# The second norm and the first group's queries of a one-core decoder kernel, in another order

## The chip, the cores and the metric

One Trainium2 chip, one of its cores. The metric is the device time of one execution in microseconds; the kernel before has a median of 811.94 us over 3 runs (811.52 to 813.64). A core has these engines, each with an instruction queue of its own: TensorE (PE, matrix products), VectorE (DVE), ScalarE (ACT), GpSimd (POOL) and SyncE (SP, which here only issues DMAs). They wait for one another on semaphores.

## The reference

One decoder layer on x of shape 16 x 64 x 512 (16 sequences of 64 tokens, 1024 tokens in all), with three parts:

```
x = x + attn(layernorm(x))        # here attn(h) = h + a softmax mix over the 16 sequences, per channel
x = x + xattn(layernorm(x), ctx)  # 32 query heads, 8 key/value heads of 128, RMS norm on queries and keys
x = x + moe(layernorm(x))         # 16 experts, 4 per token, and a shared one

q = rmsnorm(h @ Wq.T); k = rmsnorm(ctx @ Wk.T); v = ctx @ Wv.T
out = softmax(q k^T / sqrt(128) + mask) v @ Wo.T
```

The change lies at the seam of the first and second parts: the second layernorm, the transposes of its rows, and the projection of the first of eight groups of heads.

## The kernel before, in words

Products of 32-bit values are made of three products of 16-bit halves (hi x hi, hi x lo, lo x hi). So nearly every operand is split: ACT writes a high part (a 16-bit copy), then DVE or POOL subtracts it and writes the low part. Both must be there before PE can run the three products. A projection of 128 rows of weights against 512 tokens has 4 chunks, so it is 12 matmuls (`product`, L1740).

**First part, until about 56 us.** x lies as `xh`: 128 partitions (2 channel halves x 64 positions) by 16 sequences by 256 channels. DVE adds the messages of the first attention (L1236), and from the fourth of eight on `x1_done` allows more; statistics of the rows follow (L1242, L1246, L1155). PE swaps the halves' statistics by a small matmul (L2073); meanwhile it projects keys (`project_k`) and the first half of the values (`project_v(0, 0, 6, ...)`, L2070 and L2075) of group 0.

**Second norm.** ACT computes the scales (L736, L738). Then ACT normalises the rows of sequences 1, 3, ..., 11 (`ACT_ROWS`, L749) and DVE the ten others (`DVE_ROWS`, L1191) into `h2`. PE transposes them, two sequences to a tile of 128 tokens, 8 tiles (`transpose_rows`, L1817 to L1827): tile t waits for rows 2t and 2t + 1, and from t = 4 on for the low part of tile t - 4, because four PSUM banks are used in turn. ACT writes the high part (`transposed_hi`), DVE the low part (`transposed_lo`, L1252).

**First group.** `iteration(-1, False, True)` on PE (L1976 on) has 8 units u of queries: head u // 2 and half u % 2 of the tokens, in bank 4 + u % 2. Unit u >= 2 waits until the low part of unit u - 2 has been made from the same bank (`q_split`, L1865). Before unit 0 it waits for 4 low parts of tiles, before unit 1 for 8. After the units PE projects the second half of the values (L2023), then sums squares. The sums of the key squares, which give the keys' scale, come before unit 0 (L2079, half 0) and behind it (L2009, half 1), both in bank 7.

On ACT a unit is `q_parts` (L826): the query's high part (L830), its square (L834), the square's high part (L836). Beside the units each step k of the first group holds one piece of an expert weight that is split and written to `w_split` in DRAM (`first_hi(4 + k)`, L922), and the rest of the key path is laid into steps by hand:

```
L950  if k == 1: k_scale(p, 1, 7)            # ACT
L952  if k in (3, 4): k_hi_part(p, k - 3)
L954  if k == 7: v_hi_part(p, 1, 7)
L1407 if k in (1, 2): key_norm(p, k - 1)     # DVE, each behind q_lo_part and pre_lo(4 + k)
L1409 if k in (4, 5): key_lo(p, k - 4)
L1411 if k == 7: v_lo_part(p, 1, 7)
```

`k_scale` (two ACT operations) of half 0 stands before the units (L1042). DVE's step is `q_lo_part` (L1277), then the low part of the weight piece (`pre_lo`, L1362), then the key's piece. POOL makes the low part of the squares (L622). It starts its key squares (L628) only when all ten rows of DVE are done (L673).

**After the first group.** `iteration(0, ...)` begins on PE with `scores(0, 0)`, which waits for all 8 low parts of the queries and for both low parts of the keys (`k_split`, L1845, L1846), then a second part of the query sums (`sum_q_squares`, L1993), then the other scores and the 8 units of group 1. ACT goes from its last piece to the weights of group 1 (`wq_chunk`, L759), to `q_rms` (L887, waits for the query sums), to eight operations on loads in `reg_h` (L911, L913) and to the units of group 1.

**SP** issues in the order of its code: stores of pieces 0 to 3 (L416), loads of pieces 4 to 7 (L443), four moves of x from `xh` into `x_res` (L449, 2 MB in pieces of 1 KB, wait for `x1_done` 8), the next group's query and key/value weights (`query_weights(1)`, L421 and L423, 1 MB and 0.5 MB), then, when all 8 tiles are transposed (L452, since the pieces go to `reg_h`, where `h2` lies), the loads of pieces 8 to 11 (L402), then the stores of pieces 4 to 7. ACT's `first_hi(8)` waits for the load of piece 8 and for the store of piece 4 (L918, L920).

## Time and profile before

| | us |
|---|---|
| median of 3 runs (lowest, highest) | 811.94 (811.52, 813.64) |
| the profiled execution | 814.55 |
| its span, first to last instruction | 812.7 |
| PE busy | 779.1 (96%) |
| DVE, POOL, ACT busy | 591.8, 542.1, 516.9 |

Times below are microseconds from the start of the span. The profile lists, for each instruction, its engine, its line, its output and inputs, its start and length; a row of the timeline merges neighbours of one kind (xN). A number in square brackets is the time that the engine stood idle before the row and what ended it. Matmuls overlap: one of 512 columns is listed as 0.38 us long and the next starts 0.216 later. DVE and ACT operations overlap by some 0.1 us in the same way. "PEclk" or "clock" is TensorE's granted clock, 1.00 for full speed. "SPq" is the issue of DMAs on SyncE.

### The profile page before, as it was taken

How to read it: one execution, taken by the hardware profiler on the slowest of the kernel's cores; microseconds unless marked ns; L12 is line 12 of the kernel's file. 1: busy time of each engine (PE TensorE's matmuls, PEld its weight loads, DVE VectorE, ACT ScalarE, POOL GpSimd, SP SyncE). 2: the span in 40 equal slices, each digit the busy share in tenths (PEclk: the TensorE clock that was granted, in tenths of full speed). 3: DMA queues.
4: the chain of work that ended last, by engine and by line, in shares of the span. 5: the costliest groups of instructions: out<-in, count | busy, mean ns of one | idle time of the engine just before them, and what ended most of it. 6: DMA issues, size and time to landing. Idle time of an engine off the chain costs nothing.

```text
span 812.7 us, 21596 instructions
## 1 busy us (share of the span) xinstructions
PE 779.1 (96%) x7887; PEld 444.1 (55%) x7887; DVE 591.8 (73%) x1023; ACT 516.9 (64%) x968; POOL 542.1 (67%) x428
## 2 busy tenths in 40 slices
PE   6799999999999999999999999989998999999997
PEld 2674645645645645645655655744545655555553
DVE  5787895595685685686686677699688767676678
ACT  3798987487587587578487588446334565554551
POOL 6853496796896896896986977953163665654532
PEclk9899999999999999999999999999999999999999
DMA  8029426416517507507506515446325557577894
GB/s 330 15 88 294 164 75 229 139 52 232 157 39 234 165 25 233 174 7 249 166 24 232 167 41 156 140 148 234 129 59 216 195 195 267 202 276 257 273 400 159
DMA packets 50661, 138.94 MB, mean 171 GB/s; under 512 B 6176, under 2 KB 8224, under 8 KB 46240
## 3 DMA queue, kind: packets, MB, share of 16 engines
q1 hardware_dynamic: 43600, 116.93, 43.4%
q0 software_dynamic: 6400, 20.98, 7.6%
q8 instruction: 48, 0.79, 0.4%
q14 instruction: 21, 0.17, 0.1%
q10 hardware_dynamic: 592, 0.08, 0.1%
HBM read 96.02 MB, written 39.85 MB: 167 GB/s over the span
## 4 chain that ended last, share of the span: by engine, by line
PE 78%; ACT 6%; DVE 4%; DMA 4%; POOL 3%; issue 2%; SPq 2%; DVEq 0%; ACTq 0%; POOLq 0%
PE ps L1740 50%; PE ps L2190 15%; PE ps L1959 3%; DMA y_rows<-reg_h,to_row 2%; PE ps L2180 2%; PE ps L1945 2%; PE ps L1900 1%; PE ps L2251 1%; DMA w_split<-stage 1%; PE ps L2205 1%; PE ps L1757 1%; DMA ring_mem<-in_x_half 1%; SPq L449 1%; POOL ring_mem L608 1%; PE ps L2192 1%
## 5 line engine op out<-in xcount | busy, mean ns | idle before, releaser
L1740 PE MATMUL ps<-wo_hi,reg_b 128*128 128x512 f16 x448 | 142.4, 379 | 0.5 <-DVE ring_mem L1286 0.2
L2190 PE MATMUL ps<-ring_mem,reg_h 128*64 x480 | 117.0, 380 | 5.3 <-DVE kv L1637 2.3
L701 POOL DMA_INDIRECT y_rows<-reg_h,to_row x40 | 65.8, 1644 | 80.1 <-ACT reg_h L1113 73.6
L2192 PE MATMUL ps<-kv,reg_h 128*64 128x512 f16 x480 | 117.1, 380 | 0.0
L660 POOL TENSOR_SCALAR reg_h<-reg_h 128x512 f32<-128x512 f32 x56 | 95.4, 1704 | 32.5 <-ACT reg_h L911 32.3
L664 POOL TENSOR_TENSOR reg_h<-reg_h 128x512 f16<-128x512 f32 x84 | 108.7, 1294 | 4.7
L1740 PE MATMUL ps<-hT_hi,wq_hi 128*128 128x512 f16 x256 | 97.1, 379 | 1.1 <-DVE ring_mem L1277 0.9
L1740 PE MATMUL ps<-hT_lo,wq_hi 128*128 128x512 f16 x256 | 97.0, 379 | 0.0
L1740 PE MATMUL ps<-hT_hi,wq_lo 128*128 128x512 f16 x256 | 97.0, 379 | 0.0
L622 POOL TENSOR_TENSOR ring_mem<-kv,ring_mem 128x512 f16<-128x512 f32 x64 | 80.3, 1254 | 23.6 <-ACT ring_mem L836 23.6
L1740 PE MATMUL ps<-wo_lo,reg_b 128*128 128x512 f16 x224 | 84.9, 379 | 0.0
L2190 PEld LDWEIGHTS ps<-ring_mem,reg_h 128*64 128x64 f16 x480 | 47.6, 110 | 49.6 <-issue 18.0
L1740 PEld LDWEIGHTS ps<-wo_hi,reg_b 128*128 128x128 f16 x448 | 43.7, 98 | 50.3 <-issue 2.0
L1326 DVE TENSOR_TENSOR reg_b<-ps,reg_b 128x1024 f16<-128x1024 f32 x28 | 34.1, 1218 | 47.6 <-ACT reg_b L861 47.5
L1277 DVE TENSOR_TENSOR ring_mem<-ps,ring_mem 128x512 f16<-128x512 f32 x64 | 43.8, 684 | 29.1 <-ACT kv L834 28.5
L1334 DVE SCALAR_TENSOR_TENSOR x_res<-ps,x_res 128x512 f32<-128x512 f32 x64 | 43.7, 682 | 27.0 <-PE ps L1740 27.0
L2190 PE MATMUL ps<-ring_mem,wkv_st 128*64 x240 | 58.4, 379 | 1.8 <-ACT wkv_st L1105 1.8
L911 ACT ACTIVATE reg_h<-reg_h 128x512 f16<-128x512 f32 x84 | 51.9, 620 | 12.4 <-DMA reg_h<-in_wgu 8.2
L2192 PE MATMUL ps<-kv,wkv_st 128*64 128x512 f16 x240 | 58.4, 379 | 0.0
L608 POOL TENSOR_TENSOR ring_mem<-ring_mem,mask_sb 128x512 f32<-128x512 f32 x32 | 40.4, 1284 | 25.1 <-DVE ring_mem L1286 25.1
L697 POOL DMA_INDIRECT hT_hi<-h_rows,from_row x40 | 39.0, 974 | 19.7 <-issue 12.7
L830 ACT ACTIVATE ring_mem<-ps 128x512 f16<-128x512 f32 x64 | 38.0, 594 | 21.6 <-PE ps L1740 21.6
(343 smaller groups left out, 2017.2 us busy)
## 6 DMA issues: line engine op xcount, KB each, us to landing
ring_mem<-w_split SPq DMA_DIRECT2D x16, 1536.0 KB
w_split<-reg_h SPq DMA_DIRECT2D x88, 256.0 KB, 2.1
reg_h<-in_wgu SPq DMA_DIRECT2D x58, 256.0 KB, 3.6
stage<-in_wq SPq DMA_DIRECT2D x8, 1024.0 KB, 8.6
stage<-in_wo SPq DMA_DIRECT2D x8, 1024.0 KB, 6.7
reg_h<-in_wd SPq DMA_DIRECT2D x30, 256.0 KB, 3.2
wkv_st<-in_wkv SPq DMA_DIRECT2D x8, 512.0 KB, 9.3
ring_mem<-in_x_half SPq DMA_DIRECT2D x8, 256.0 KB, 6.5
```

The source lines that it names most:

```text
L608: pool.tensor_tensor(t, t, mask_sb[:, :].unsqueeze(1).to_broadcast([P, 8, S]), ALU.add).then_inc(masked, 1)
L622: pool.tensor_tensor(sq_lo[:, j // 2, 8 * th:8 * th + 8, j % 2, :], sq32[:, u % 2, :].rearrange("p (b s) -> p b s", s=S), w, ALU.subtract) ...
L660: pool.tensor_scalar(st, st, WS, None, ALU.mult).then_inc(pre_scaled_pool, 1)
L664: pool.tensor_tensor(hl[:, 1, :], st, hl[:, 0, :], ALU.subtract).then_inc(pre_split, 1)
L697: pool.indirect_dma_start(h_slot[r % KC], None, h_rows, bass.IndirectOffsetOnAxis(ap=from_row[:, r - 1:r], axis=0)).then_inc(gathered[r % ...
L701: pool.indirect_dma_start(y_rows, bass.IndirectOffsetOnAxis(ap=to_row[:, r - 1:r], axis=0), y[r % 2], None).then_inc(scattered[r % 2], 16)
L911: act.activation(pre_hl[us][:, 0, :], pre_st[us], ACT.Copy, scale=WS).then_inc(pre_hi, 1)
L1277: dve.tensor_tensor(q_lo[:, j // 2, 8 * th:8 * th + 8, j % 2, :], ps[:, 4 + u % 2, :].rearrange("p (b s) -> p b s", s=S), q_hi[:, j // 2, ...
L1334: dve.scalar_tensor_tensor(x_res[:, t, :], ps[:, 2 + t % 2, :], 1.0 / (WS * WS), x_res[:, t, :], ALU.mult, ALU.add).then_inc(o_added, 1)
L1740: last = pe.matmul(dst, lhsT(c), rhs(c), start=(m == 0), stop=(m == n - 1))
L2190: pe.matmul(dst[0:TS, :], x[:, 0:TS], ring[:, bass.ds(at + w, BANK)], start=(first and n == 0), stop=(stop and n == 2))
L2192: last = pe.matmul(dst[TS:P, :], x[:, TS:P], upper_w[r % 2][:, w:w + BANK], start=(first and n == 0), stop=(stop and n == 2))
```

## The change

- **Rows in two halves.** ACT normalises rows 1, 4, 6, then makes the high parts of tiles 0 to 3, then rows 9, 12, 14 and tiles 4 to 7; DVE in the same way with rows 0, 2, 3, 5, 7 and 8, 10, 11, 13, 15. PE transposes tiles 0 to 3, and tiles 4 to 7 behind the first query unit. POOL's key squares wait for five rows instead of ten.
- **Units by token halves.** Units 0 and 1 of group 0 are heads 0 and 1 on the first 512 tokens, units 2 and 3 the same heads on the others, and so on (`unit`). Unit 0 has its 12 matmuls in another order (8 that need only high parts of the tokens, then 4 with low parts).
- **Values ahead.** The second half of the values is projected before the first transposes (one tile of four) and behind them (the other three), instead of behind the units. Their high and low parts go from step 7 to step 1.
- **Key path.** The sums of key squares go behind units 1 and 2, in banks 0 and 1. ACT's key scales go to steps 2 and 3, its key high parts to steps 5 and 6; DVE's key norms to steps 3 and 4, its key low parts to steps 6 and 7.
- **SP.** The next group's weights and the loads of pieces 8 to 11 come before the moves of x.

```diff
--- before.py
+++ after.py
@@ -73,11 +73,23 @@
 BANK = 512
 ACT_ROWS = range(1, 12, 2)
 DVE_ROWS = [n for n in range(B) if n not in ACT_ROWS]
+SECOND_ACT_ROWS = ((1, 4, 6), (9, 12, 14))
+SECOND_DVE_ROWS = ((0, 2, 3, 5, 7), (8, 10, 11, 13, 15))
 
 
 def rows_to(rows, n):
 
     return sum(m <= n for m in rows)
+
+
+def second_rows_to(rows, n):
+
+    return max(i + 1 for i, m in enumerate(itertools.chain(*rows)) if m <= n)
+
+
+def unit(p, u):
+
+    return (2 * (u // 4) + u % 2, u % 4 // 2) if isinstance(p, int) and p == 0 else (u // 2, u % 2)
 
 
 def sums_to(t, k=None):
@@ -442,17 +454,17 @@
                 src = wgu[c // ITEMS, :, c % ITEMS, :] if c % ITEMS < KC else wd[c // ITEMS, :, c % ITEMS - KC, :]
                 sp.dma_start(first_st[q], src).then_inc(pre_in[q], 16)
 
+            query_weights(1)
+            sp.wait_ge(hT_ps, NT)
+            for q in range(SLOTS):
+                sp.wait_ge(pre_in[q], 32)
+                pre_load(0, 2 * SLOTS + q)
             x_pairs = xh.rearrange("p (t b) l -> p t b l", b=2)
             sp.wait_ge(x1_done, 8)
             for half in range(2):
                 for b in range(2):
                     sp.dma_start(x_res[b * S:(b + 1) * S, :, half * HALF:(half + 1) * HALF],
                                  x_pairs[half * S:(half + 1) * S, :, b, :]).then_inc(x1_moved, 16)
-            query_weights(1)
-            sp.wait_ge(hT_ps, NT)
-            for q in range(SLOTS):
-                sp.wait_ge(pre_in[q], 32)
-                pre_load(0, 2 * SLOTS + q)
             for q in range(SLOTS, 2 * SLOTS):
                 first_store(q)
             for q in range(SLOTS):
@@ -616,7 +628,7 @@
                                    ALU.subtract).then_inc(shifted, 1)
 
             def square_lo(p, u):
-                j, th = u // 2, u % 2
+                j, th = unit(p, u)
                 pool.wait_ge(sq_hi_done, ev(p, 8, u))
                 w = sq_hi[:, j // 2, 8 * th:8 * th + 8, j % 2, :]
                 pool.tensor_tensor(sq_lo[:, j // 2, 8 * th:8 * th + 8, j % 2, :],
@@ -670,7 +682,7 @@
 
             for q in range(SLOTS):
                 first_lo(q)
-            pool.wait_ge(h2_dve, len(DVE_ROWS))
+            pool.wait_ge(h2_dve, len(SECOND_DVE_ROWS[0]))
             k_square_lo(0, 0)
             k_square_lo(0, 1)
             iteration(-1, False, True)
@@ -824,7 +836,7 @@
                     "p (k c) -> p k c", c=P), ACT.Copy).then_inc(hT_hi_done, 1)
 
             def q_parts(p, u):
-                j, th = u // 2, u % 2
+                j, th = unit(p, u)
                 bank = ps[:, 4 + u % 2, :]
                 act.wait_ge(q_ps, ev(p, 8, u))
                 act.activation(q_hi[:, j // 2, 8 * th:8 * th + 8, j % 2, :],
@@ -947,11 +959,11 @@
                         first_hi(SLOTS + k)
                     if not att:
 
+                        if k in (2, 3):
+                            k_scale(p, k - 2, k - 2)
+                        if k in (5, 6):
+                            k_hi_part(p, k - 5)
                         if k == 1:
-                            k_scale(p, 1, 7)
-                        if k in (3, 4):
-                            k_hi_part(p, k - 3)
-                        if k == 7:
                             v_hi_part(p, 1, 7)
                     if att and proj and 2 <= k < 6:
                         soft_exp(i, k - 2)
@@ -1035,11 +1047,14 @@
             k_parts(0, 0)
             k_parts(0, 1)
             ln_rstd(2, slice(0, B))
-            normalise_rows(2, lambda n: h2[:, n, :], h2_act)
-            for t in range(NT):
-                transposed_hi(0, t, t % 4)
+            act.wait_ge(shift_ready, 2)
+            for part in range(2):
+                for n in SECOND_ACT_ROWS[part]:
+                    act.activation(h2[:, n, :], xh[:, n, :], ACT.Identity, scale=rstd[:, n:n + 1],
+                                   bias=shift_ln[:, n:n + 1]).then_inc(h2_act, 1)
+                for t in range(4 * part, 4 * part + 4):
+                    transposed_hi(0, t, t % 4)
             v_hi_part(0, 0, 6)
-            k_scale(0, 0, 7)
             iteration(-1, False, True, True)
             with act.Fori(0, G - 2) as i:
                 iteration(i, True, True, True)
@@ -1180,18 +1195,21 @@
             dve.wait_ge(consts, 22)
             row_scales(1, 7)
 
-            def normalise_rows(count, bank, dst, done):
+            def row_shifts(count, bank):
 
                 dve.wait_ge(rstd_ready, count)
                 both = ps[:, bank, 2 * B:4 * B].rearrange("p (n s) -> p n s", s=2)
                 dve.scalar_tensor_tensor(shift_ln[:, :], both[:, :, 0], -0.5, rstd[:, 0:B],
                                          ALU.mult, ALU.mult).then_inc(shift_ready, 1)
                 dve.wait_ge(shift_ready, count)
-                for n in DVE_ROWS:
-                    dve.tensor_scalar(dst(n), xh[:, n, :], rstd[:, n:n + 1], shift_ln[:, n:n + 1],
-                                      ALU.mult, ALU.add).then_inc(done, 1)
-
-            normalise_rows(1, 7, lambda n: hq[:, :, n], h1_dve)
+
+            def normalise_row(n, dst, done):
+                dve.tensor_scalar(dst, xh[:, n, :], rstd[:, n:n + 1], shift_ln[:, n:n + 1],
+                                  ALU.mult, ALU.add).then_inc(done, 1)
+
+            row_shifts(1, 7)
+            for n in DVE_ROWS:
+                normalise_row(n, hq[:, :, n], h1_dve)
             dve.memset(used[:, 0:PRE], 1.0)
             dve.tensor_copy(count16[:, :], count_up[:, :])
             dve.tensor_scalar(below[:, :], count_up[:, :], row_no[:, 0:1], None, ALU.is_gt)
@@ -1265,13 +1283,16 @@
             row_scales(2, 0)
             dve.wait_ge(small_in, 80)
             then(dve.tensor_tensor(wqk[:, :], norm_sb[:, 0:1], norm_sb[:, 1:2], ALU.mult))
-            normalise_rows(2, 0, lambda n: h2[:, n, :], h2_dve)
-            for t in range(NT):
-                transposed_lo(0, t, t % 4)
+            row_shifts(2, 0)
+            for part in range(2):
+                for n in SECOND_DVE_ROWS[part]:
+                    normalise_row(n, h2[:, n, :], h2_dve)
+                for t in range(4 * part, 4 * part + 4):
+                    transposed_lo(0, t, t % 4)
             v_lo_part(0, 0, 6)
 
             def q_lo_part(p, u):
-                j, th = u // 2, u % 2
+                j, th = unit(p, u)
                 dve.wait_ge(q_hi_done, ev(p, 8, u))
                 dve.wait_ge(sq32_done, ev(p, 8, u))
                 dve.tensor_tensor(q_lo[:, j // 2, 8 * th:8 * th + 8, j % 2, :],
@@ -1404,11 +1425,11 @@
                         pre_lo(SLOTS + k)
                     if not att:
 
-                        if k in (1, 2):
-                            key_norm(p, k - 1)
-                        if k in (4, 5):
-                            key_lo(p, k - 4)
-                        if k == 7:
+                        if k in (3, 4):
+                            key_norm(p, k - 3)
+                        if k in (6, 7):
+                            key_lo(p, k - 6)
+                        if k == 1:
                             v_lo_part(p, 1, 7)
                     if att and 3 <= k < 7:
                         normalise(i, k - 3)
@@ -1816,8 +1837,8 @@
 
             def transpose_rows(t):
 
-                pe.wait_ge(h2_dve, rows_to(DVE_ROWS, 2 * t + 1))
-                pe.wait_ge(h2_act, rows_to(ACT_ROWS, 2 * t + 1))
+                pe.wait_ge(h2_dve, second_rows_to(SECOND_DVE_ROWS, 2 * t + 1))
+                pe.wait_ge(h2_act, second_rows_to(SECOND_ACT_ROWS, 2 * t + 1))
                 if t >= 4:
                     pe.wait_ge(hT_split, t - 3)
                 cols = ps[:, t % 4, :].rearrange("p (h k b c) -> p k b h c", h=2, k=2, b=2)
@@ -1858,7 +1879,7 @@
                 last.then_inc(s_ps, 1)
 
             def project_q(p, u):
-                j, th = u // 2, u % 2
+                j, th = unit(p, u)
                 if u == 0:
                     pe.wait_ge(wq_split, p * KC + KC)
                 if u >= 2:
@@ -1869,6 +1890,17 @@
                         parts(lambda c: wq_hi[:, c, heads], lambda c: wq_lo[:, c, heads],
                               lambda c: hT_hi[:, c, cols], lambda c: hT_lo[:, c, cols]),
                         range(KC)).then_inc(q_ps, 1)
+
+            def project_first_q():
+                pe.wait_ge(wq_split, KC)
+                pe.wait_ge(hT_hi_done, NT // 2)
+                for c in range(KC):
+                    for w in (wq_hi, wq_lo):
+                        pe.matmul(ps[:, 4, :], w[:, c, 0:HD], hT_hi[:, c, 0:BANK], start=(c == 0 and w is wq_hi), stop=False)
+                pe.wait_ge(hT_split, NT // 2)
+                for c in range(KC):
+                    last = pe.matmul(ps[:, 4, :], wq_hi[:, c, 0:HD], hT_lo[:, c, 0:BANK], start=False, stop=(c == KC - 1))
+                last.then_inc(q_ps, 1)
 
             def project_k(p, th):
                 if th == 0:
@@ -1997,16 +2029,21 @@
 
                             if att:
                                 pe.wait_ge(v_split, ev(i, 2, u))
-                            else:
-                                pe.wait_ge(hT_split, 4 * u + 4)
+                        if not att and u == 2:
+                            pe.wait_ge(hT_split, NT)
                         if att and u == 6:
                             if first:
                                 pe.wait_ge(v_split, 2)
                             transpose_pair(i, 0)
-                        project_q(p, u)
                         if not att and u == 0:
-                            pe.wait_ge(ln_k, 1)
-                            sum_k_squares(p, 1, 7)
+                            project_first_q()
+                            for t in range(NT // 2, NT):
+                                transpose_rows(t)
+                        else:
+                            project_q(p, u)
+                        if not att and u in (1, 2):
+                            pe.wait_ge(hT_split, NT // 2 + u)
+                            sum_k_squares(p, u - 1, u - 1)
                     if att:
                         heads_pair(i, 0)
                         transpose_pair(i, 2)
@@ -2019,8 +2056,6 @@
                         transpose_pair(i, 4)
                         sum_k_squares(p, 0, 4)
                     else:
-                        pe.wait_ge(ln_k, 2)
-                        project_v(p, 1, 7)
                         sum_q_squares(p, 3, range(NT // 2))
                 if att and not proj:
 
@@ -2073,10 +2108,12 @@
             pe.matmul(ps[:, 0, 0:2 * B], swap[:, :], mv[:, :, :].rearrange("p n s -> p (n s)"),
                       start=True, stop=True).then_inc(swapped, 1)
             project_v(0, 0, 6, range(2, 4))
+            pe.wait_ge(x1_done, 4)
+            project_v(0, 1, 7, range(1))
             pe.wait_ge(var_ready, 2)
-            for t in range(NT):
+            for t in range(NT // 2):
                 transpose_rows(t)
-            sum_k_squares(0, 0, 7)
+            project_v(0, 1, 7, range(1, 4))
             iteration(-1, False, True)
             iteration(0, True, True, first=True)
             with pe.Fori(1, G - 2) as i:
```

## Rows read from the trace of the kernel before

**Rows 1.** The page: TensorE busy, and the chain by engine.
```profile
PE 779.1 (96%) x7887; PEld 444.1 (55%) x7887; DVE 591.8 (73%) x1023; ACT 516.9 (64%) x968; POOL 542.1 (67%) x428
...
PE 78%; ACT 6%; DVE 4%; DMA 4%; POOL 3%; issue 2%; SPq 2%; DVEq 0%; ACTq 0%; POOLq 0%
```

**Rows 2.** Timeline, PE, 58 to 100: start, us, what, [idle before, releaser].
```profile
58.52 2.10 PE L1826 MATMUL ps<-ident,reg_h 128*128 128x128 f32 x16 [1.32 <-DVE reg_h L1191]
...
62.18 2.42 PE L1826 MATMUL ps<-ident,reg_h 128*128 128x128 f32 x16 [1.56 <-DVE hT_lo L1252]
...
89.66 0.94 PE L1900 MATMUL ps<-ones,ring_mem 128*128 128x1 f16 x32
90.46 0.86 PE L1740 MATMUL ps<-kv,ring_mem 128*128 128x64 f16 x24
...
94.15 0.38 PE L1740 MATMUL ps<-hT_hi,wq_hi 128*128 128x512 f16 x1
...
99.98 0.39 PE L1740 MATMUL ps<-hT_hi,wq_hi 128*128 128x512 f16 x1 [0.48 <-DVE ring_mem L1277]
```

**Rows 3.** Chain of waits, 72 to 130: start, us, what.
```profile
72.74 8.59 DMA w_split<-stage
...
84.38 5.46 PE ps L1740 x60
...
127.95 2.59 PE ps L1740 x12
```

**Rows 4.** Timeline, ACT, 57 to 98.
```profile
57.77 3.06 ACT L749 ACTIVATE reg_h<-ring_mem,shift_ln,rstd 128x256 f32<-128x256 f32 x6 [0.31 <-DVE shift_ln L1187]
...
67.66 0.60 ACT L830 ACTIVATE ring_mem<-ps 128x512 f16<-128x512 f32 x1 [0.70 <-PE ps L1740]
...
81.41 0.63 ACT L922 ACTIVATE reg_h<-reg_h 128x512 f16<-128x512 f32 x1 [0.77 <-DMA w_split<-stage]
...
88.83 0.61 ACT L922 ACTIVATE reg_h<-reg_h 128x512 f16<-128x512 f32 x1
...
92.43 0.28 ACT L887 ACTIVATE rq<-ps,eps_q 128x32 f32<-128x32 f32 x1
...
98.07 0.57 ACT L830 ACTIVATE ring_mem<-ps 128x512 f16<-128x512 f32 x1
```

**Rows 5.** Windows: stretch; busy PE, PEld, DVE, ACT, POOL; clock; DMA share; GB/s.
```profile
62.60:72.70 10.10, 10.10 (x53) 5.09 (x52) 6.83 (x11) 8.46 (x16) 2.20 (x3) 1.00 1.10 223
72.70:81.40 8.70, 8.37 (x39) 3.50 (x38) 6.73 (x8) 7.81 (x15) 4.04 (x4) 1.00 0.98 374
67.66:89.35 21.69, 21.26 (x129) 10.45 (x128) 15.41 (x19) 19.56 (x36) 8.54 (x8) 1.00 0.89 277
```

**Rows 6.** Timeline, DVE, 57 to 90.
```profile
57.77 3.32 DVE L1191 TENSOR_SCALAR reg_h<-ring_mem,rstd,shift_ln 128x256 f32<-128x256 f32 x10
...
82.07 0.69 DVE L1362 SCALAR_TENSOR_TENSOR reg_h<-reg_h 128x512 f16<-128x512 f32 x1 [1.30 <-ACT reg_h L922]
...
89.47 1.23 DVE L1362 SCALAR_TENSOR_TENSOR reg_h<-reg_h 128x512 f16<-128x512 f32 x1 [0.42 <-ACT reg_h L922]
```

**Rows 7.** Timeline, POOL, at 89.
```profile
89.00 1.16 POOL L622 TENSOR_TENSOR ring_mem<-kv,ring_mem 128x512 f16<-128x512 f32 x1 [1.41 <-ACT ring_mem L836]
```

**Rows 8.** Timeline of SyncE (the moves); landing of the four loads before them.
```profile
59.27 6.19 SPq L449 DMA_DIRECT2D x_res<-ring_mem  x4
...
DMA to landing us min/median/max: 3.3/3.6/4.4
```

**Rows 9.** Windows, as rows 5: two stretches without a matmul, and behind.
```profile
10.02:12.51 2.49, 0.00 (x0) 0.00 (x0) 2.44 (x14) 0.00 (x0) 2.38 (x3) 0.99 1.07 456
12.51:15.50 2.99, 2.99 (x9) 1.34 (x10) 1.49 (x8) 1.15 (x3) 1.55 (x1) 0.50 0.93 397
33.23:37.20 3.97, 0.00 (x0) 0.00 (x0) 3.63 (x6) 3.87 (x8) 3.97 (x3) 0.90 0.00 0
37.20:43.10 5.90, 5.86 (x48) 5.89 (x50) 3.72 (x6) 5.68 (x10) 1.35 (x1) 0.50 0.01 4
```

## The prediction

> **What bounds the kernel now.** The page comes first: TensorE (PE) is busy for 96% of the span and makes 78% of the chain that ended last [rows 1]. A microsecond is therefore won only where PE stands still, or where another engine holds it up. I then read PE in order of time around the edit [rows 2]. It stands still 1.32 us before the first row transposes (it waits for the first rows of the second norm) and 1.56 us before the second sixteen (it waits for VectorE's first low part). These 2.9 us are what the halving is aimed at. From 64.9 us PE runs eight units of queries, the values of the second half, the sums of squares and the scores, until the next group's queries begin at 94.15.
>
> The chain of waits over the same stretch [rows 3] does not run through those stalls: it goes through a store into w_split (72.74, 8.59 us) and the last block of queries and values (84.38). So ACT has to be read next [rows 4]. It starts the first unit at 67.66, waits 0.77 us at 81.41 for that store to land, begins its last expert piece of the stage at 88.83 (done with it at 89.35), and begins the next group's units at 98.07. In the 21.7 us from 67.66 ACT is busy 19.6 [rows 5]. PE and ACT run nearly level, and what the change does to ACT and DVE decides.
>
> **Part 1, the rows in halves (PE, ACT, DVE).** DVE does 10 rows in 3.3 us, 0.32 apart, ACT 6 in 3.0, 0.5 apart [rows 4, 6]. The first four tiles now need only 5 and 3 of them. They are ready by 59.4, and PE still cannot start its transposes before 58.5, since the first tile needs the same two rows as before; it ends the sixteen at 60.6, as now. The values moved here fill what follows: 48 small matmuls cost the chain block of 60 (5.46, to the end of its last) less a unit of 12, up to the sums' start at 89.66: 89.66 - 84.38 - 2.59 = 2.7 [rows 2, 3]; a quarter (0.7) fits into the old 1.32 us stall, the rest runs 60.6 to 62.6. By then ACT, free of rows at 59.25, has made the four high parts (61.4) and DVE the low ones (62.4). PE's first unit runs 62.6 to 65.2 (2.59 for twelve [rows 3]), the second sixteen transposes 65.2 to 67.4 (2.2 [rows 2]). **PE gains the whole 2.9 us here** in work done.
>
> ACT does not. After its second three rows, at 62.7, it waits for the second transposes: they come only behind the values and the first unit. Its high parts run 65.8 to 68.0 (0.5 each, paced by PE's 0.55 a tile), then the first value part (0.5), so its first unit starts at 68.5 instead of 67.66: **0.8 late**.
>
> **Part 2, the order in the units.** PE's work is the same but for its place: 67.4 + 7 units of 2.59 + four key-sum matmuls of the same width (0.22 each by 2.59 / 12) = 86.4 for the last unit's end if nothing holds it, against 89.66 for the same work now. ACT's share grows: of the 21.7 us to its last first-group piece (89.35) it waits about 1.8 and works or turns round 19.85. Now the first key scale (two operations on 512 elements, each 0.6 like its neighbours [rows 4]) and the second value part (0.5) lie inside too. That is 21.6 us, from 68.5 to **90.1**, with no idle time left. It is 0.75 later than today's 89.35.
>
> DVE is behind ACT: the last piece's low part can start only at 90.1. Beside GpSimd's subtraction such an operation takes 1.23 us, alone 0.69 [rows 6, 7]; its neighbour in time is the 1.23 row, which I take, 0.69 being the other bound. The second key's low part was at step 5 of the loop and is now at step 7, *behind* this operation: another 0.6. So the keys are complete at 90.1 + 1.15 + 0.6 = 91.85, and the scores, which wait for both key halves, start at 91.9 where today they start at 90.46 [rows 2]. **This is the step that takes the gain back.** PE's 2.9 us reappear as a stall between the query sums and the scores.
>
> **Part 3, SyncE's queue.** Moved ahead of the four moves of x are the two weight loads for the next group and the four loads into reg_h. The latter wait for the eighth transpose, now 67.4 (today 64.6); the x moves are queued behind this wait, and behind the moves the stores of units 4 to 7. The moves take 6.2 us to issue today [rows 8], the last loads before them take 3.3 to 4.4 us to land, and then follow 10.1 us at 223 GB/s (2 MB in all: the moves), against 374 GB/s once they are through [rows 5, 8]. In the new order the loads are issued by 69.2, through by some 71.8, the moves through at 81.9, the first store (0.25 MB) and its completion at about 82.4. ACT needs it at 68.5 plus five units, both key scales and the value part: 81.7 to 81.9. So it waits 0.6 in place of the 0.77 that I have already taken out; bounds: 0 (the loads land sooner), and 2.8: today the store lands 22.1 after the moves begin to issue (59.27 to 72.74 + 8.6), with 2.5 MB of weights and loads between, 6.7 us at 374 GB/s; 69.2 + 22.1 - 6.7 = 84.6. The Trainium skill, DMA: Bandwidth & Descriptors, in Bandwidth, gives on-chip moves a ceiling of 435 GB/s and says that small pieces do not slow them. By that rule the 2 MB would be through in half the time, the wait would be 0 and the sum 0.6 lower; the trace shows 223, and the trace decides here.
>
> The moves of x themselves are needed only when DVE enters the next group (95 us) and have landed by 82: nothing, hidden under the units. Loads for the next group, and the output weights, are issued 0.3 to 1.2 us later than now and used 1.6 later: nothing. GpSimd's key squares start at 59.5 beside DVE's PSUM reads instead of behind ten rows and end before the next rows: nothing; were that wrong, the rows behind would slip by 0.5 and still be ready before 65.2.
>
> **Sum.** ACT's last piece 90.1 + 0.6 = 90.7; keys 92.5; first scores, then the query sums (0.7 + 0.8) to 94.0; ACT's query scale then at 94.05 against 92.43 [rows 4]: **+1.6**. From there ACT has the weights of the next group and eight operations on loads, without a wait up to 98.07, and PE's third unit waits for what follows (99.98, after 0.48 idle [rows 2]), so the 1.6 goes through: the next units start at 99.7. Behind it PE is full up to the end of the attention and every later step shifts. On the profiled execution (814.55 us, span 812.7) that gives 816.15; this execution lies 2.6 above the median of the runs, 811.94, so the forecast is 811.94 + 1.6 = **813.5 us**, +0.2%. A measurement of this kernel can tell 0.3% (2.4 us) from no change, so this counts as no change. Its own range, from the bounds (the store's wait 0 or 2.8, the low part 0.69 or 1.23, ACT's start 0.3 off either way), is 812.2 to 816.0. Chance 0.45.
>
> **Rivals.**
> *The clock falls in the new stall (0.22).* PE now stands still from the first query sums, about 89.2, to 92.5: 3.3 us. The granted clock fell from full to half (2.4 to 1.2 GHz) twice: at the end of 2.49 us without a matmul, and toward the end of 3.97 us [rows 9]; after the 1.56 us stall it was full [rows 5]. Mine lies between the two that fell. Half rate lasted 3.0 and 5.9 us. It would lie on the scores and sums, 3.7 us of PE of which the first 1.5 hold up ACT's query scale: +1.5 to +3, by half the longer row 3.0. Taken at 2.2: 813.5 + 2.2 = 815.7, slower than today by 0.46%. It decides once the stall is above about 2.5 us. The Trainium skill, TensorE: Matmul & The Clock Gate, in What's actually happening, makes half rate the default and activity what lifts it; the first two rows agree. Against: low work from 89.66 to 94.15 today keeps the clock.
>
> *The moves of x hold the store longer (0.13).* The upper bound above: ACT waits 2.8 at its ninth piece, 2.2 more than taken: 815.7. It decides when the store lands later than 83.3, the wait then being 1.4 and the whole +2.4. For it: the moves are slow, and the store lies behind all of them. Against: they have the queue to themselves.
>
> *The keys come in time (0.15).* If ACT keeps today's end of 89.35 or earlier (its waits of 1.8 vanish and its work overlaps better) and DVE does the last key part in a gap, the scores start with the last query part, at 89.5 against 90.46: 811.0. For it: PE is 3.2 us ahead. Against: the order on DVE is fixed.
>
> *PE is the bound throughout (0.05).* The 2.9 us are kept: 809.0. Against: ACT's 21.6 us of work.
>
> **Range and chances.** 810.6 to 816.4 holds the first, third and fourth cases and most of the clock's. Slower by over 0.3%: 0.18 of the clock case, 0.09 of the store's, 0.03 of the forecast's own tail, 0.30. Faster by over 0.3%: the last case and a rest, 0.06. Within: 0.64.
>
> **What would show it.** Right: ACT's first unit at about 68.5 and its last piece near 90.5; no PE idle before the second transposes; PE idle about 3 us before the first scores, released by the key's low part; the scores at 92 to 93; the next group's first query part 1 to 2 us later than 98.07. The store: ACT's wait at its ninth piece, 0 to 2.8. Clock: half rate in a slice behind the stall. Wrong: scores before 90.5, no stall there, or ACT's first unit before 67.7.

## The result, and the profile after

The changed kernel takes 817.65 us (median of 7 runs, 814.92 to 820.09), the kernel before, in as many runs beside it, 813.64 us (811.52 to 815.87). The recorded ratio is 1.0062, with a 95% interval of 1.0039 to 1.0085: **slower by 0.6%, 3.2 to 6.9 us** (the quotient of the two medians alone is 1.0049, 4.0 us). The forecast was 813.5 us, to be counted as no change, with a range of 810.6 to 816.4.

| | before | after |
|---|---|---|
| the profiled execution, us | 814.55 | 817.65 |
| its span | 812.7 | 815.8 |
| first row normalised (ACT) | 57.77 | 61.10 |
| mean granted clock, whole span | 0.994 | 0.985 |

The two traces begin the second norm 3.3 us apart, although next to nothing ahead of it was changed (one tile of values, the 12 matmuls of which end before the norm's first rows). The clock was at half rate for longer there (0.83 on average over the first 61.10 us against 0.91 over the first 57.77). The stage, which reaches from the second norm to the next group's queries, is therefore read from its own start. A time with a plus sign, here and below, counts from the first normalised row on ScalarE.

The timeline of ACT after, to be laid beside [rows 4]:

```profile
61.10 1.58 ACT L1053 ACTIVATE reg_h<-ring_mem,shift_ln,rstd 128x256 f32<-128x256 f32 x3 [0.31 <-DVE shift_ln L1202]
...
71.25 0.65 ACT L842 ACTIVATE ring_mem<-ps 128x512 f16<-128x512 f32 x1
...
86.71 0.63 ACT L934 ACTIVATE reg_h<-reg_h 128x512 f16<-128x512 f32 x1 [2.07 <-DMA w_split<-stage]
...
94.22 0.61 ACT L934 ACTIVATE reg_h<-reg_h 128x512 f16<-128x512 f32 x1
...
98.80 0.29 ACT L899 ACTIVATE rq<-ps,eps_q 128x32 f32<-128x32 f32 x1 [1.89 <-PE ps L1932]
...
104.46 0.58 ACT L842 ACTIVATE ring_mem<-ps 128x512 f16<-128x512 f32 x1
```

The first unit starts at +10.15 (+9.89 before), the ninth piece of expert weights (L934, the fifth of this stage) at +25.61 after 2.07 us of waiting for the store (+23.64, 0.77), the last piece at +33.12 (+31.06), the query scale at +37.70 (+34.66), the next group's first unit at +43.36 (+40.30). **The stage is 3.1 us longer.** Two thirds of this are there at the ninth piece.

PE after, beside [rows 2], and DVE ahead of the scores:

```profile
61.84 1.94 PE L1847 MATMUL ps<-ident,reg_h 128*128 128x128 f32 x16 [1.00 <-DVE reg_h L1207]
...
68.22 1.91 PE L1847 MATMUL ps<-ident,reg_h 128*128 128x128 f32 x16
...
89.39 0.39 PE L1761 MATMUL ps<-hT_hi,wq_hi 128*128 128x512 f16 x1 [1.79 <-DVE ring_mem L1298]
...
96.84 1.09 PE L1761 MATMUL ps<-kv,ring_mem 128*128 128x64 f16 x24 [2.96 <-DVE kv L1367]
```

```profile
94.86 1.23 DVE L1383 SCALAR_TENSOR_TENSOR reg_h<-reg_h 128x512 f16<-128x512 f32 x1 [0.24 <-ACT reg_h L934]
96.02 0.68 DVE L1367 TENSOR_TENSOR kv<-kv 128x512 f16<-128x512 f32 x1
```

The stall before the second transposes is gone; before the first, 1.00 us of 1.32 is left. In their place PE waits 1.79 us before the last unit (DVE and ACT are late because of the store) and 2.96 us before the scores, for the key's low part (L1367), which DVE makes behind the last piece's (L1383). The scores start at +35.74; before, at +32.69.

SyncE after, then the landing of its four loads (L414), then windows (stretch; busy PE, PEld, DVE, ACT, POOL; clock; DMA share; GB/s):

```profile
70.16 0.81 SPq L414 DMA_DIRECT2D reg_h<-in_wgu  x2
71.01 0.90 SPq L414 DMA_DIRECT2D reg_h<-in_wd  x2
71.96 6.11 SPq L466 DMA_DIRECT2D x_res<-ring_mem  x4
78.11 4.27 SPq L428 DMA_DIRECT2D w_split<-stage  x2
```

```profile
DMA to landing us min/median/max: 3.4/4.4/5.1
```

```profile
69.00:71.00 2.00, 2.00 (x16) 1.44 (x15) 1.51 (x3) 2.00 (x5) 0.00 (x0) 1.00 0.53 211
77.00:79.00 2.00, 2.00 (x11) 0.94 (x10) 1.77 (x3) 1.94 (x5) 1.06 (x1) 1.00 1.12 222
...
98.00:99.00 1.00, 1.00 (x37) 1.00 (x35) 1.00 (x2) 0.20 (x1) 0.00 (x0) 0.50 0.68 209
100.00:101.00 1.00, 1.00 (x28) 1.00 (x26) 1.00 (x2) 1.00 (x3) 0.00 (x0) 0.65 0.14 41
```

The moves begin at +10.86, behind a stretch in which the DMA engines are half idle (0.53). The last of the loads ahead of them lands at +15.4, the last move at +24.9 (222 GB/s in between), the store that ACT waits for at +25.5. Behind the 2.96 us stall the clock is at half rate from 97.3 to 100.7.

### The profile page after: what moved, and what is told of

Same layout as the page of the kernel before. It is cut to its first block, busy times and chain, and to the rows that moved or that the text cites. A ratio compares the mean times of both kernels' runs of the same rounds, so it can differ in the third digit from the quotient of the medians.

```text
span 815.8 us, 21598 instructions
## 1 busy us (share of the span) xinstructions
PE 781.9 (96%) x7887; PEld 448.9 (55%) x7887; DVE 591.4 (72%) x1023; ACT 516.0 (63%) x968; POOL 542.1 (66%) x428
## 4 chain that ended last, share of the span: by engine, by line
PE 76%; ACT 5%; DVE 5%; POOL 5%; DMA 4%; issue 4%; SPq 0%; DVEq 0%; POOLq 0%; ACTq 0%
PE ps L1761 46%; PE ps L2227 16%; PE ps L1991 2%; PE ps L2217 2%; PE ps L1977 2%; POOL ring_mem L634 1%; POOL ring_mem L620 1%; DMA y_rows<-reg_h,to_row 1%; PE ps L1932 1%; DMA stage<-in_wq 1%; PE ps L2288 1%; PE ps L1778 1%; DMA w_split<-stage 1%; PE ps L2242 1%; POOL reg_h L676 1%
```

## The experiments

The kernels were measured in three sets, each on a chip of its own: 10 to 12 runs of each against 33 to 35 runs of the kernel before on the same chip (medians 811.74, 814.48 and 814.12 us), which the ratio is to. The first set is changed_again, moves_first, key_first and values_behind; the second before_again, clock_filled, moves_first_keys_earlier and loads_first_alone; the third the other four. The row of the first changed trace is the result above, 7 runs against 7. The plus times are the starts in one trace each: ACT's first unit; ACT's ninth piece, with its wait for the store; PE's first scores; ACT's first unit of the next group. "Second scale" is the query scale of the next group on ACT, from where on all traces advance in step (62.7 us a group).

| kernel | ratio (95%) | first unit | ninth piece (wait) | scores | next units | second scale |
|---|---|---|---|---|---|---|
| before | | 9.89 | 23.64 (0.77) | 32.69 | 40.30 | 84.50 |
| before_again | 1.0008 (0.9982, 1.0033) | 9.89 | 23.98 (1.10) | 33.03 | 40.64 | 84.89 |
| changed, first trace | 1.0062 (1.0039, 1.0085) | 10.15 | 25.61 (2.07) | 35.74 | 43.36 | 87.88 |
| changed_again | 1.0047 (1.0021, 1.0072) | 10.15 | 26.44 (2.91) | 37.58 | 45.72 | 89.78 |
| moves_first | 1.0046 (1.0023, 1.0070) | 10.16 | 23.99 (0.45) | 34.13 | 42.53 | 86.60 |
| key_first | 1.0033 (1.0010, 1.0056) | 10.15 | 25.97 (2.43) | 35.75 | 43.69 | 87.71 |
| values_behind | 1.0056 (1.0031, 1.0081) | 11.98 | 27.67 (2.31) | 37.80 | 45.56 | 89.61 |
| clock_filled | 1.0047 (1.0028, 1.0065) | 10.15 | 25.66 (2.12) | 35.80 | 43.14 | 87.17 |
| moves_first_keys_earlier | 1.0017 (0.9999, 1.0035) | 10.15 | 23.45 (0) | 31.92 | 39.53 | 83.59 |
| loads_first_alone | 1.0040 (1.0023, 1.0057) | 9.89 | 26.69 (3.83) | 37.43 | 45.04 | 89.28 |
| weights_first_alone | 1.0069 (1.0041, 1.0097) | 9.90 | 26.08 (3.21) | 36.82 | 44.44 | 88.46 |
| weights_late_alone | 0.9996 (0.9980, 1.0012) | 9.89 | 22.77 (0) | 32.41 | 40.17 | 84.51 |
| all_repaired | 0.9999 (0.9979, 1.0018) | 10.16 | 23.46 (0) | 31.93 | 40.15 | 84.37 |
| values_spread | 0.9974 (0.9957, 0.9991) | 9.28 | 22.58 (0) | 31.05 | 39.05 | 83.07 |

**changed_again.** No edit.

> The changed kernel once more, as the base of this set. In its first trace ScalarE waits 2.07 us at the ninth expert piece, PE stands still 2.96 us before the first scores, and the clock is at half rate from about 97.3 to 100.6 behind that. Theory (three parts: the late store, the key's low part behind the last piece's, the clock): the same three again, and 3 to 5 us over the kernel before. Rival (the first stage, whose code is unchanged but whose clock fell for longer in that trace, makes the difference by chance): 0 to 2 us over the kernel before, with a shorter half rate in the first 50 us.

The loss is no chance of the first trace: this one begins the norm at 56.84, earlier than the kernel before, and its stage is longer still (+45.72). The store's wait was 2.91 us, and the clock fell twice: at the wait of 2.63 us before the last unit (half rate 85.4 to 88.8) and at the one of 3.53 us before the scores (92.2 to 99.1). The rival falls.

**before_again.** The kernel before, unchanged.

> The kernel before once more, for a second trace of its stage and as a measure of what two builds of one kernel differ by. Both theories: ratio within 0.2% of 1; the next group's first unit about 40.3 us after the first normalised row, no half rate between there and the norm. If the clock falls here too, the falls in the changed kernel are no effect of the change.

Its stage repeats within 0.4 us, without a fall of the clock between the norm and the next units. Its whole span was 816.3 us all the same (812.7 in the first trace), with 2.5 us more ahead of the norm. One execution says little here; the stage and the medians do.

**moves_first.** SyncE's old order in the changed kernel:

```diff
-            query_weights(1)
-            sp.wait_ge(hT_ps, NT)
-            ... pre_load(0, 2 * SLOTS + q)
             ... the four moves of x
+            query_weights(1)
+            sp.wait_ge(hT_ps, NT)
+            ... pre_load(0, 2 * SLOTS + q)
```

> The changed kernel with SyncE's old order: the four moves of x ahead of the weights and of the loads of pieces 8 to 11. Theory (the store behind the moves holds ScalarE): the wait at the ninth piece goes from 2.07 to under 0.5, the last piece and the scores come about 1.5 us earlier, the stall before the scores stays near 3 us, time 1.5 to 2 us under the changed kernel. Rival (the store's wait is covered by PE and DVE, and the key path alone decides): under 0.5 us gained. Second rival (the loads of the pieces are needed early): ScalarE waits for a load instead, and nothing is gained.

The wait fell to 0.45 us and the scores came 1.6 us earlier than in the first changed trace (3.4 earlier than in the second); the stall before them stayed at 2.96, and the clock fell in it, for 6.8 us (89.6 to 96.4). The ratio did not move (1.0046, against 1.0047 for changed_again in the same set), though this trace is 1.3 us ahead at the second scale; the intervals overlap too far to tell the two apart.

**key_first.** In step 7 of DVE:

```diff
                     if not att:
+                        if k == 7:
+                            key_lo(p, 1)
                         pre_lo(SLOTS + k)
...
-                        if k in (6, 7):
-                            key_lo(p, k - 6)
+                        if k == 6:
+                            key_lo(p, 0)
```

> The changed kernel with one swap on DVE: in step 7 the second key's low part stands ahead of the last piece's low part. Theory: the scores, which wait for it, start 1.6 us earlier, PE's stall before them shrinks from 2.96 to about 1.4 us, and with a stall that short the clock stays at full rate behind it; 1.6 us without and up to 3 us with the clock. Rival (the last query part or the query sums hold the scores anyway): the stall shrinks by less than 0.5 us.

```profile
85.70 0.39 PE L1763 MATMUL ps<-hT_hi,wq_hi 128*128 128x512 f16 x1 [2.15 <-DVE ring_mem L1298]
...
92.81 1.42 PE L1763 MATMUL ps<-kv,ring_mem 128*128 128x64 f16 x24 [1.88 <-DVE kv L1367]
```

Against its own last piece (+34.78) the scores start 0.97 us later, in the changed kernel 2.62: the swap brings 1.65, as expected. The clock, though, fell both at the wait before the last unit, which the store makes (86.0 to 89.5), and again behind the scores (92.9 to 96.3), after a stall of 1.88 us. My expectation of full rate was wrong.

**values_behind.** The three tiles and the one tile of values go back behind the units, their parts back to step 7:

```diff
-            project_v(0, 1, 7, range(1))
...
-            project_v(0, 1, 7, range(1, 4))
...
                     else:
+                        project_v(p, 1, 7)
                         sum_q_squares(p, 3, range(NT // 2))
```

> The changed kernel with the second half of the values back behind the eight units, and their high and low parts back in step 7. Theory (they were the work that covered PE's wait for the keys): no stall over 1.5 us before the query sums and scores, no half rate there; and ScalarE gets the second four tiles about 2 us earlier, so its first unit starts about 1 us earlier; 2.5 to 4 us under the changed kernel. Rival (PE bound: the values' place is indifferent): within 1 us of the changed kernel.

```profile
58.13 3.08 PE L1847 MATMUL ps<-ident,reg_h 128*128 128x128 f32 x16 [1.99 <-DVE reg_h L1207]
61.99 0.58 PE L1899 MATMUL ps<-hT_hi,wq_hi 128*128 128x512 f16 x1 [0.78 <-ACT hT_hi L829]
```

A miss. The stall before the scores did shrink, to 1.11 us, but without the values PE stood still 1.99 and 0.78 us around the transposes, and the clock was at half rate from 58.7 to 65.6, and once more behind the scores (96.3 to 99.7), where I had expected none. The first unit came at +11.98 instead of about +9. In this arrangement the values around the transposes are needed: with them the clock stayed full there in every trace.

**clock_filled.** Behind the first query sums of the changed kernel, on constants, never read:

```diff
                         sum_q_squares(p, 3, range(NT // 2))
+                        for _ in range(11):
+                            pe.matmul(ps[:, 2, :]..., ident16[:, :], blockmask16[:, :]..., start=True, stop=True)
```

> The changed kernel with eleven matmuls of constants (512 columns, their result is never read) on PE between the first query sums and the scores, in the stall of 3 us. Theory (ScalarE, not PE, sets the way from the scores to the next units, so the half rate there costs little): the clock stays full behind the stall, and the way from the scores to the next group's first unit, 7.62 us in the first changed trace and 8.14 in the second, goes to 7.6; at most 0.8 us gained. Rival (my forecast's clock case: half rate on scores and sums costs 1.5 to 3 us): 1.5 us or more gained between scores and next unit.

```profile
93.61 2.53 PE L2061 MATMUL ps<-blockmask,ident 128*128 128x512 bf16 x11
...
96.71 0.86 PE L1761 MATMUL ps<-kv,ring_mem 128*128 128x64 f16 x24 [0.57 <-DVE kv L1367]
```

The clock stayed full, and with the store's wait nearly as in the first changed trace (2.12, 2.07) the second scale came 0.7 us earlier; the ratio did not move (1.0047). From scores to next units it was 7.34 us against 7.62, all of the difference ahead of the query scale; from there ACT takes 5.66 us in both. So 3.4 us of half rate behind the scores cost 0.3 us here, and 0.7 by the second scale, not my 1.5 to 3. Half rate for 6.8 us goes with 8.14 (changed_again) and 8.40 us (moves_first), up to 1.1 more; but this stretch takes 7.34 to 8.00 us in traces without a fall too, so that single traces price it no closer.

**loads_first_alone.** The kernel before, with only the changed kernel's order on SyncE.

> The kernel before with only the new order of SyncE: weights and loads of pieces 8 to 11 ahead of the moves of x. Theory (the store is late because the moves wait for the eighth transpose, and this comes 2.8 us later in the changed kernel; the order alone costs little): the moves begin about 66.5 us, 8.7 after the first row, the store lands 14.7 later, ScalarE's wait at the ninth piece is 0.5 to 1.5 us (0.77 before), time within 0.2% of the kernel before. Rival (the order itself is bad, whenever the eighth transpose comes): a wait of 2 us or more, and 1.5 us or more slower.

```profile
84.63 0.63 ACT L922 ACTIVATE reg_h<-reg_h 128x512 f16<-128x512 f32 x1 [3.83 <-DMA w_split<-stage]
```

```profile
87.60 0.39 PE L1740 MATMUL ps<-hT_hi,wq_hi 128*128 128x512 f16 x1 [3.16 <-DVE ring_mem L1277]
```

```profile
66.63 6.01 SPq L454 DMA_DIRECT2D x_res<-ring_mem  x4
72.69 5.83 SPq L416 DMA_DIRECT2D w_split<-stage  x2
```

My theory fell and its rival stands: **the order alone makes the kernel slower, by 0.23 to 0.57%**, and its stage by 4.7 us at the next units. Of these 4.7, 3.05 are there at the ninth piece. The other 1.6 come between the ninth and the last piece (9.05 us, 7.42 before): the late store leaves PE standing still for 3.16 us before its last unit, and the clock falls behind that. The moves began at +8.7 as expected, but ACT had its store 18.0 us later, not 14.7. The windows from 80 on:

```profile
80.00:82.00 2.00, 2.00 (x11) 0.94 (x10) 0.69 (x1) 0.77 (x2) 1.12 (x1) 1.00 1.07 363
82.00:84.00 2.00, 2.00 (x11) 0.89 (x10) 0.00 (x0) 0.00 (x0) 0.04 (x1) 1.00 0.52 186
84.00:86.00 2.00, 0.44 (x3) 0.00 (x0) 0.71 (x2) 1.37 (x3) 0.00 (x0) 1.00 0.10 37
...
89.00:92.00 3.00, 3.00 (x10) 1.13 (x9) 2.36 (x4) 1.08 (x2) 1.17 (x1) 0.50 0.95 353
```

ACT does nothing for two microseconds while the DMA rate fades from 363 to 37 GB/s and the mean busy share of the 16 engines from 1.07 to 0.10. In that tail the last move lands at +26.0, 3.65 us behind the third (2.4 in the kernel before), and the store at +26.6.

**weights_first_alone.** The kernel before; only `query_weights(1)` goes ahead of the moves.

> The kernel before with the next group's weights ahead of the moves of x, while the loads of pieces 8 to 11 stay behind them. It halves the edit of loads_first_alone, where ScalarE waited 3.83 us at the ninth piece. Theory A (there the moves came behind the wait for the eighth transpose, at +8.7 instead of +1.5, and finish late): here they begin at about +2.5, and ScalarE's wait is 0.5 to 1.5 us. Theory B (the order of the bytes itself counts: moves right ahead of the stores are slow to finish): a wait of 2.5 us or more here too.

```profile
60.20 8.39 SPq L450 DMA_DIRECT2D x_res<-ring_mem  x4
...
75.39 0.94 SPq L416 DMA_DIRECT2D w_split<-stage  x2
```

Theory B: a wait of 3.21 us although the moves begin at +2.4. The same bytes are ahead of the store as in the kernel before, and ACT has it at +26.1 instead of +23.6 (+24.0 in before_again). From the norm to there, first in the kernel before, then here:

```profile
57.77:81.77 24.00, 21.36 (x110) 10.81 (x111) 18.13 (x30) 21.45 (x40) 8.03 (x7) 1.00 1.02 292
57.77:83.77 26.00, 23.36 (x119) 11.72 (x120) 18.14 (x30) 21.10 (x39) 8.14 (x7) 1.00 1.02 269
```

The same 7.0 MB pass, with the engines as busy (1.02), at 269 GB/s instead of 292. In windows of 1 us the rate is lowest from 60.77 to 62.77 (180 and 160 GB/s), where no packet of the moves (1 KB each) is under way yet, and from 67.77 to 68.77 (157), where they have just begun; in the kernel before no such window on the way to the store is under 200. Why the same bytes are slower in this order was not found. Here too the clock fell before the last piece (half rate 87.6 to 91.0, after a stall of 2.54 us), which took 9.11 us from the ninth.

**moves_first_keys_earlier.** moves_first, and the key path a step earlier:

```diff
-                        if k in (5, 6):
-                            k_hi_part(p, k - 5)
+                        if k in (4, 5):
+                            k_hi_part(p, k - 4)
...
-                        if k in (6, 7):
-                            key_lo(p, k - 6)
+                        if k in (5, 6):
+                            key_lo(p, k - 5)
```

> The changed kernel with the moves of x ahead of the loads, as in moves_first, and the key path one step earlier behind the norms: ScalarE's key high parts in steps 4 and 5, DVE's key low parts in steps 5 and 6. Theory (late store and late key are the two losses of the stage): counted from the first normalised row, the last piece at about +31.5 us, the scores wait only for the last query part and start at +31.8 to +32.3 (34.13 in moves_first, 32.69 in the kernel before), stall under 1.5 us, the next group's first unit at +40 to +41 (42.53, 40.30 before); time within 0.2% of the kernel before. Rival (another wait takes the place of the keys, as the query sums by way of GpSimd): scores no earlier than +33.5.

```profile
87.16 0.95 PE L1932 MATMUL ps<-ones,ring_mem 128*128 128x1 f16 x32 [0.76 <-POOL ring_mem L634]
88.91 0.87 PE L1761 MATMUL ps<-kv,ring_mem 128*128 128x64 f16 x24 [0.80 <-DVE ring_mem L1298]
```

As expected: the scores wait 0.80 us for the last query part and start at +31.92. The stage is 0.8 us shorter than before the change, and the ratio, 1.0017, is not told apart from 1. The clock fell here too, from 89.7 to 93.1, behind stalls of only 0.76 and 0.80 us.

**weights_late_alone.** The kernel before, with the weights behind the stores of pieces 4 and 5:

```diff
             ... the four moves of x
-            query_weights(1)
             sp.wait_ge(hT_ps, NT)
...
             for q in range(SLOTS, 2 * SLOTS):
                 first_store(q)
+                if q == SLOTS + 1:
+                    query_weights(1)
```

> The kernel before with one edit on SyncE: the next group's weights (1.5 MB) behind the stores of pieces 4 and 5 instead of behind the moves of x. Times counted from the first normalised row. Theory (the store of piece 4 lands late because of the bytes ahead of it in the queue, about 4 us of them being the weights): the store lands by +20, ScalarE's wait at its ninth piece (0.77 and 1.10 in two traces of the kernel before) is gone, the next group's first unit comes at +39.5 to +40 (40.30 and 40.64), 0.5 to 1 us gained, which this many runs can hardly show. Rival (the store waits for the moves of x in any order): the wait stays near 0.8.

ACT's wait is gone, the ninth piece comes at +22.77, and yet the last piece comes only 0.28 us earlier and the next units 0.13: further on ACT waits for PE's units instead. In the kernel before the store's wait was covered.

**all_repaired.** moves_first_keys_earlier with the weights late.

> The changed kernel with the moves of x first, the next group's weights behind the stores of pieces 4 and 5, and the key path one step earlier. In moves_first_keys_earlier the next units began at +39.53 and ScalarE had just no wait at its ninth piece (+23.45). Theory (that stage is then bound by ScalarE's own work): the ninth piece stays at +23.4, the next units at +39.5; within 0.2% of the kernel before. Rival (the queue still held something): next units at +39 or earlier.

The ninth piece did not move (+23.46): without the store ACT is bound by its own work there. The next units came at +40.15, 0.6 later than expected. The clock does not explain that: it fell for 3.4 us behind the scores in this trace (91.0 to 94.4) as in moves_first_keys_earlier (89.7 to 93.1). The difference is 0.2 us at the query scale and 0.4 in ACT's eight operations on loads (4.77 us, 4.36 there); its cause is open.

**values_spread.** all_repaired, with the values in other places, and their high and low parts in step 7 instead of step 1:

```diff
-                        if k == 1:
+                        if k == 7:
                             v_hi_part(p, 1, 7)
...
-            project_v(0, 1, 7, range(1))
+            project_v(0, 1, 7, range(2))
...
-            project_v(0, 1, 7, range(1, 4))
+            project_v(0, 1, 7, range(2, 3))
...
                     else:
+                        project_v(p, 1, 7, range(3, 4))
                         sum_q_squares(p, 3, range(NT // 2))
```

> As all_repaired, and the second half of the values is spread: two tiles ahead of the first transposes, one behind them, one behind the eight units. Theory (ScalarE's 2.78 us wait for the second four tiles is what is left to gain, and two small blocks of values are enough to fill PE's waits at the norm): ScalarE's first unit at +8.8 to +9.2 (10.15 in the changed kernel, 9.89 in the one before), ninth piece at +22.3, next units at +38.3 to +38.8 (40.30 before), no half rate between the norm and the scores; 1.5 to 2 us (0.2%) under the kernel before. Rival (with the values gone from there the clock falls at the norm, as in values_behind): first unit at +10 or later and nothing gained.

```profile
96.94 0.57 ACT L843 ACTIVATE ring_mem<-ps 128x512 f16<-128x512 f32 x1
```

The first unit starts at +9.28 and the next units at 96.94, +39.05: 1.25 us before those of the kernel before, and no fall of the clock in the stage. The ratio is 0.9974 (0.9957 to 0.9991), 811.5 us against 814.12. It is the only version whose whole interval lies under 1; with thirteen comparisons made, one that ends this near to 1 deserves a second measurement, which was not made. Two things were moved at once, the values and the step of their parts, and the run does not say which of them counts.

## Why the prediction was wrong

**Part 1 held.** The second transposes start without a stall, ACT waits 2.78 us for them, and its first unit starts 0.26 us late where I had 0.8.

**Part 2 held in its mechanism.** The last piece, had the store not been late, comes at +31.1 (all_repaired), where my sum gave its end as 90.1, which is +32.3 and so +31.8 for its start: 0.7 too much. The key's place was the loss named. From the last piece's start to the scores it is 2.62 us after and 0.82 with the keys a step earlier: **1.8 us**, forecast 1.75.

**Part 3 is the step that failed.** I put the order on SyncE at an ACT wait of 0.6 us in place of 0.77, so at nothing lost. The wait was 2.07 us in the first trace and 2.12 to 2.91 in four others with this order. Taken against +31.1, the last piece is 2.0 us late in the first trace by it. The moves began at +10.86, a little before my +11.4, and ACT had the store 14.7 to 15.6 us later, not 13.2. What was mis-sized is the time that the loads just ahead of the moves take. I had them through at +14.0, 2.6 us behind their issue, against my own rows, where such loads took 3.3 to 4.4; the last one took 5.1 and landed at +15.4, in changed_again 6.3, at +16.7. The moves and the store behind them then took about as long as reckoned. So the store landed at +25.5 instead of +24.6, and ACT was ready for it at +23.5, 0.4 sooner than I had it.

A second error lies under this one: I never asked what the order does on the kernel before. There it makes a wait of 3.83 us, above my bound of 2.8, because the bound moved today's 22.1 us along and took off the missing bytes at 374 GB/s, which supposes that bytes cost the same in every order. The two orders with weights ahead of the moves, on the kernel before, show that they do not. The rule of the Trainium skill on on-chip moves (DMA: Bandwidth & Descriptors, in Bandwidth) would have made the wait 0; the trace shows 222 GB/s again.

The scores thus start 3.05 us later than before: 31.9 (keys in time, no store) + 2.0 + 1.8 = 35.7, against 32.69. Forecast: +34.7. Another 0.4 us was lost in the sum behind them: I took 1.55 us from the scores to the query scale, where the kernel before shows 1.97 (90.46 to 92.43) and the changed one 1.96.

What the ratios carry and what only traces carry is to be kept apart. That the order alone costs time is shown by the ratios of loads_first_alone and weights_first_alone. That the late store and the late key together make the loss is shown by all_repaired, which has neither (at most 1.0018, where the changed kernel has at least 1.0021). How the loss divides between the two in the changed kernel is read from traces alone: the intervals of moves_first and key_first overlap those of the changed kernel.

**The clock's rival happened, at another price.** I gave it 0.22 and 2.2 us. Half rate did follow the stall, in both changed traces, but in the first it costs 0.3 to 0.7 us behind the scores, since from the query scale on ACT sets the pace. It costs more where I had not looked, at the wait before the last unit that the late store makes. In changed_again the clock fell there, and from the ninth to the last piece it took 8.5 us instead of 7.5; in the two kernels with the order alone 9.1 instead of 7.4. The Trainium skill (TensorE: Matmul & The Clock Gate, in What's actually happening) makes half rate the default and activity what lifts it; the falls at PE's stalls of 1.88 to 3.53 us agree. The rows are not clean, though: the clock also fell behind stalls of 0.76 and 0.80 us (moves_first_keys_earlier), and stayed full behind 1.79 (the first changed trace) and 1.85 (clock_filled). My mark of 2.5 us, above which the rival was to decide, did not hold: key_first fell behind 2.15 and 1.88.

**The store's rival** (0.13) is the nearest to what happened, the wait of 2.1 to 2.9 against its 2.8, together with the clock. I had added them as alternatives; they are one chain, because the late store makes a stall in which the clock falls. That, and the median of 811.94 from three runs, which lay 1.7 us under that of seven, put the result outside the range.

## What to carry to other kernels

A DMA that is moved in a queue moves the landing of what stands behind it, and here not in proportion to bytes: try the order alone on the old kernel before you price it. When work is taken from behind a stage to fill a hole ahead of it, look at what it covered there; here it covered a key path that had been allowed to be late. And stalls that follow from one another are to be added in one case, not set side by side as rivals.

## What the runs showed of the hardware that was not expected

- Moves from SBUF to SBUF in pieces of 1 KB ran at about 220 GB/s (223 before, 222 after), the loads and stores behind them at 374 and 381. With 1.5 MB of loads just ahead of them, ACT had the store behind them 2.1 to 2.5 us later than with the same loads just behind them (+26.1 against +23.6 and +24.0).
- A queue's rate fades at its end, from 363 to 37 GB/s over some 4 us (loads_first_alone), and in that fade the last move landed 3.65 us behind the one before it, not 2.4.
- The granted clock fell to half rate behind PE stalls of 1.88 to 3.53 us, in three traces behind shorter ones (1.11 and 0.80), for 3.4 or 6.8 us. It fell also for 3.4 us near 540 or 620 us in nine of the fourteen traces, where all run the same code, and for different lengths in the first 46 us: 10.2 us in the first trace of the kernel before and 17.0 in the second, whose norm begins 2.5 us later.
